# Graph attention on Trainium2: VectorE adds the edge rows to keys and values in one wide instruction, and its four dot products move behind the addition of a finished step's sum

## The chip, the cores and the metric

The kernel runs on one core of one Trainium2 chip. The metric is the device time of one execution in microseconds (us). A core has a matrix engine (TensorE, PE in the rows; its weight loads are PEld), a vector engine (VectorE, DVE), a scalar engine (ScalarE, ACT), GpSimd (POOL), SyncE (SP, used here for DMA issue) and 16 DMA engines. The engines run in order, each on its own queue, and meet through semaphores.

## What is computed

A graph of 6250 nodes and 100000 edges, sorted by destination, passes through one weighted neighbour sum with a residual and a layer norm, and then through two attention convolutions. All of the change lies in the convolutions, which compute, with H = 4 heads of C = 64 channels:

```
q, k, v = x @ Wq + bq, x @ Wk + bk, x @ Wv + bv      # per node
e = edge_attr @ We                                   # per edge
kj = k[src] + e
vj = v[src] + e
logits = einsum('ehc,ehc->eh', q[dst], kj) / sqrt(C)
m = segment_max(logits, dst)
ex = exp(logits - m[dst])
denom = segment_sum(ex, dst)
agg = segment_sum(vj * (ex / denom[dst])[:, :, None], dst)
```

## The kernel before

The program runs five passes one after the other with a barrier between them: the weighted edge pass, a node pass, the attention edge pass of the first convolution (e1), a second node pass, the attention edge pass of the second convolution (e2), and a last node pass. Only `edge_pass_attention` is touched; it is called twice.

An attention pass walks over 832 **steps** of 128 edges each, all edges of a step having their destination in one block of 128 nodes. 26 steps (BATCH) form a **batch** whose softmax is done together, and there are 32 batches. The pass is a software pipeline written out by hand: each engine has its own loop over i, and each step's work is spread over two visits.

In loop round i, the **front** of step i is done:

- GpSimd gathers the 512 numbers of key and value of each edge's source into one of six buffers `kv` (line 1303). It may overwrite a buffer once VectorE's value addition of six steps earlier is done. Every fourth step it also makes the selection matrices `pick` of four steps (line 1294).
- TensorE makes the edge row e (lines 1315 and 1316, in three steps of four; in the fourth it comes ready from memory as `made`) into one of two PSUM banks, and q of the destinations (line 1325) into one of two others.
- VectorE, in `logits(i)`, adds e to the keys (line 1416) and then to the values (line 1420), each 128x256, and makes four dot products of 64 numbers, one for each head (line 1428; each is a product and a short read of the accumulator). The sum of the keys goes to one of two places of `kvj`. The sum of the values goes to one of NV = 44 places, because it is needed much later; so the value addition waits until ScalarE has weighed the step 44 earlier (`weighed`).

The **back** is done LAG = 42 rounds later, when the softmax of the batch is known. In round i ScalarE makes step i-42's mask (lines 1561 and 1567) and weighs its four heads of values (line 1571). TensorE's `sum_up` (line 1366) multiplies the mask by the weighed values of step i-43, into one of two PSUM banks. VectorE's `add_sums` (line 1510) adds the sum of step i-44 to its node block in `acc`. Where that step begins a batch, it first rescales the block (lines 1504 and 1507), and this waits for the same sum. In the text below a step's place is its round modulo 26; since 44 is 18 modulo 26, the rescaling falls on place 18.

Between these, all engines share the batch softmax, by place: a transpose of the logits on TensorE and a scaled copy on ScalarE (place 0, line 1543), two scans on VectorE (place 2, lines 1433 and 1436), further copies and scans (places 6 and 10), the subtraction of the maxima on VectorE (place 12, line 1474), for which ScalarE's exponential waits (place 12, line 1546), and a last transpose and copy (place 14, line 1551). So ScalarE waits for VectorE's `lr` at place 12 of every batch.

VectorE's loop is

```
for i in range(END):
    if i < T:
        logits(i)
    if LATE <= i - LAG < T:
        late_part(i - LAG)
    if 0 <= i - LAG - 2 < T:
        add_sums(i - LAG - 2)
```

followed by the first convolution's skip product (one block of nodes at a time, 49 times in e1), the batch softmax and a small scale update. TensorE's loop runs, in round i: edge row of step i+1, q of step i+1 (which waits for the dots of step i-1), a skip product if due, the softmax transposes, `sum_up(i-43)`.

Of the kernel before, what the change touches and what calls it, by code (L numbers as in the profile page):

```python
# [7 lines left out]
P = 128  # L8
D = 256
H = 4  # L10
C = D // H
# [3 lines left out]
BATCH = 26  # L15
QUAD = 4
# [13 lines left out]
ALU = mybir.AluOpType  # L30
# [1099 lines left out]
def edge_pass_attention(nc, name, k, t, s, w_edge, edge_rows_made, kv_rows, pens, locals16, singles, skip_of):  # L1130
# [10 lines left out]
    T, batches = s.steps, s.batches  # L1141
    LATE = T - LAG
    ident, acc = k["ident"], k["acc"]
    with Phase(nc, name) as ph:
# [17 lines left out]
        if skip_of is not None:  # L1162
# [20 lines left out]
            ph.sems("kv_got", NG), ph.sems("ea_got", NE), ph.sems("runs_got", 2), ph.sems("spots_got", 2))  # L1183
        made_got = ph.sems("made_got", 2)
        w_got, cleared, ones_set = ph.sem("w_got"), ph.sem("cleared"), ph.sem("ones_set")
        e_done, q_done, kj_done, vj_done, dots_done, picked, apart_done = (
            ph.sem(n) for n in ("e_done", "q_done", "kj_done", "vj_done", "dots_done", "picked", "apart_done"))
        flat_done, lr_done, fw_done, mx_inner = (ph.sem(n) for n in ("flat_done", "lr_done", "fw_done", "mx_inner"))
        ends_up, rows_in, outs_done = (ph.sem(n) for n in ("ends_up", "rows_in", "outs_done"))
        across, ends_down, mx_done, less_max = (ph.sem(n) for n in ("across", "ends_down", "mx_done", "less_max"))  # L1190
# [8 lines left out]
        def step_of(a):  # L1199

            return a // (QUAD - 1) * QUAD + a % (QUAD - 1)
# [23 lines left out]
        with nc.Block() as block:  # L1225

            @block.sync
            def _(e):
                tile = Numbers(e, f"{name}_tile", k["tile_row"], s.tiles - 1)

                def load_attrs(a):
                    n = tile.at(step_of(a))
                    if a >= NE:
                        e.wait_ge(e_done, a - NE + 1)
                    e.dma_start(ea[:, a % NE, :], t["attr_tiles"][bass.ds(n, 1), :, :].rearrange("o k c -> (o k) c")
                                ).then_inc(ea_got[a % NE], 16)

                def load_made(c):
                    if c >= 2:
                        e.wait_ge(vj_done, (c - 1) * QUAD)  # L1240
                    e.dma_start(made[:, c % 2, :], edge_rows_made[c * P:(c + 1) * P, :]).then_inc(made_got[c % 2], 16)

                def load_spots(c):
                    if c >= 2:
                        e.wait_ge(picked, c - 1)
                    e.dma_start(spots[:, c % 2, :], locals16[c * QUAD:(c + 1) * QUAD, :].rearrange("s c -> (s c)").unsqueeze(0)
                                .to_broadcast([P, QUAD * P])).then_inc(spots_got[c % 2], 16)

                def load_runs(j):
                    if j == 0:  # L1250
                        e.wait_ge(cleared, 8)
                    if j >= 2:
                        e.wait_ge(mx_done, j - 1)
                    for h in range(H):
                        e.dma_start(pen[ROWS * h + 1:ROWS * h + 1 + BATCH, j % 2, :],
                                    pens[j * BATCH:(j + 1) * BATCH, 0:P + 1]).then_inc(runs_got[j % 2], 16)
                    for way in range(2):
                        e.dma_start(by_head(over[:, j % 2, way, :]),
                                    singles[way:way + 1, j * BATCH:(j + 1) * BATCH].unsqueeze(1)
                                    .to_broadcast([1, H, BATCH])).then_inc(runs_got[j % 2], 16)  # L1260

                e.dma_start(we[:], w_edge).then_inc(w_got, 16)
                load_spots(0)
                for a in range(NE - 1):
                    load_attrs(a)
                load_made(0)
                load_spots(1)
                if skip:
                    skip.load_weights(e)
                for i in range(T):  # L1270
                    c, at = i // QUAD, i % QUAD
                    a = c * (QUAD - 1) + at
                    if at < QUAD - 1 and a + NE - 1 < FRESH:
                        load_attrs(a + NE - 1)
                    if at == QUAD - 1 and c + 1 < s.quads:
                        load_made(c + 1)
                    if i % QUAD == 0 and i // QUAD + 2 < T // QUAD:
                        load_spots(i // QUAD + 2)
                    if i % BATCH == 0:
                        load_runs(i // BATCH)  # L1280
                    if i in due:
                        skip.load(e, due[i] + 1)
                        skip.store(e, due[i])
                if skip:
                    skip.all_stored(e)

            @block.gpsimd
            def _(e):
                def pick_rows(c):

                    e.wait_ge(spots_got[c % 2], 16 * (c // 2 + 1))
                    if c >= 2:
                        e.wait_ge(q_done, (c - 1) * QUAD)
                    e.tensor_scalar(pick[:, c % 2, :], spots[:, c % 2, :], k["own"][:, 0:1], None, ALU.is_equal).then_inc(picked, 1)  # L1294

                e.memset(kvj[:], 1.0).then_inc(ones_set, 1)
                for i in range(T):
                    u = i % NG
                    if i % QUAD == 2:
                        pick_rows(i // QUAD)  # L1300
                    if i >= NG:
                        e.wait_ge(vj_done, i - NG + 1)
                    e.indirect_dma_start(out=kv[:, u, :], out_offset=None,  # L1303
                                         **rows_of(kv_rows, k["src"][:, i:i + 1])).then_inc(kv_got[u], 16)
                e.wait_ge(ones_set, 1)

            @block.tensor
            def _(e):
                chosen = Numbers(e, f"{name}_chosen", k["q_row"], (s.blocks - 1) * D)

                def edge_product(a):
                    e.wait_ge(ea_got[a % NE], 16 * (a // NE + 1))
                    if a >= 2:
                        e.wait_ge(vj_done, step_of(a - 2) + 1)
                    e.matmul(pe_e[a % 2][:, 0:D], ea[:, a % NE, 0:P], we[:, 0, :], start=True, stop=False)  # L1315
                    e.matmul(pe_e[a % 2][:, 0:D], ea[:, a % NE, P:2 * P], we[:, 1, :],  # L1316
                             start=False, stop=True).then_inc(e_done, 1)
# [74 lines left out]
            def _(e):  # L1392
# [7 lines left out]
                if skip:  # L1400
                    skip.make_bias(e)

                def logits(i):
                    j, r = i // BATCH, i % BATCH + 1
                    e.wait_ge(kv_got[i % NG], 16 * (i // NG + 1))
                    c, at = i // QUAD, i % QUAD
                    if at < QUAD - 1:
                        a = c * (QUAD - 1) + at
                        e.wait_ge(e_done, a + 1)
                        edge = pe_e[a % 2][:, 0:D].rearrange("p (h c) -> p h c", h=H)  # L1410
                    else:
                        e.wait_ge(made_got[c % 2], 16 * (c // 2 + 1))
                        edge = made[:, c % 2, :].rearrange("p (h c) -> p h c", h=H)
                    if i >= 2:
                        e.wait_ge(dots_done, i - 1)
                    e.tensor_tensor(kvj[:, i % 2, :, 0:C], kv[:, i % NG, 0:D].rearrange("p (h c) -> p h c", h=H), edge,  # L1416
                                    ALU.add).then_inc(kj_done, 1)
                    if i >= NV:
                        e.wait_ge(weighed, i - NV + 1)
                    e.tensor_tensor(kvj[:, 2 + i % NV, :, 0:C], kv[:, i % NG, D:].rearrange("p (h c) -> p h c", h=H), edge,  # L1420
                                    ALU.add).then_inc(vj_done, 1)
                    e.wait_ge(kj_done, i + 1)
                    e.wait_ge(q_done, i + 1)
                    if j >= 2:
                        e.wait_ge(flat_done, j - 1)
                    for h in range(H):
                        hs = slice(h * C, h * C + C)
                        dot = e.tensor_tensor_reduce(kvj[:, i % 2, h, 0:C], kvj[:, i % 2, h, 0:C], pe_q[i % 2][:, hs], 1.0, 0.0,  # L1428
                                                     ALU.mult, ALU.add, logit[:, j % 2, h, r:r + 1])
                    dot.then_inc(dots_done, 1)  # L1430
# [88 lines left out]

                for i in range(END):  # L1520
                    if i < T:
                        logits(i)
                    if LATE <= i - LAG < T:
                        late_part(i - LAG)
                    if 0 <= i - LAG - 2 < T:
                        add_sums(i - LAG - 2)
                    if i in due:
                        skip.add(e, due[i])
                    j, step = step_at(i)
                    if j is not None:  # L1530
                        softmax(j, step)
                    if 0 <= i - LAG < T:
                        drop_less_one(i - LAG)
# [120 lines left out]
```

## Time and profile before

| | |
|---|---|
| Median of 3 runs | 4820.88 us (4820.83 to 4821.61) |
| The profiled execution's own time | 4832.06 us |
| Its span, first to last instruction | 4830.3 us |
| Busy: TensorE (matmul) | 4189.2 us, 87% |
| Busy: VectorE | 3989.0 us, 83%, 22772 instructions |
| Busy: ScalarE | 2982.2 us, 62% |
| Busy: GpSimd | 3116.4 us, 65% |
| First and last key addition (line 1416) | 1368.7 and 4646.8 us |

The shares are means over six passes. The two attention passes fill most of the span behind 1368.7 us, so the table by stretches of time says more than the totals. The recorded duration of a VectorE instruction is longer than its share of the engine: the next one begins before the last record ends, so the cost of an instruction in a full queue is the distance between two starts.

### The profile page before, as it was taken

Reading aid. Unit: us, or ns where it says so; the run is one execution under the profiler, and the core shown is the slowest. Engines: PE = TensorE matmul, PEld = TensorE weight load, DVE = VectorE, ACT = ScalarE, POOL = GpSimd, SP = SyncE. Lnnn points to the kernel's source line nnn. Section 1 sums busy time; section 2 is a strip of 40 time slices with the busy share of each in tenths; the row PEclk is TensorE's granted clock in tenths of the full one; section 3 lists DMA queues with packets and bytes.
Section 4 is the critical chain, followed back from the end, with each engine's and each line's share of the span. In section 5 each row is a group of like instructions: output and inputs, shape, how many; then the busy total and the mean of one; then the engine's idle time right before and its main releaser. Section 6 shows DMA issues by size and latency. Waiting matters only on the chain. (4 is left out here: it accounts for less than half of the span.)

```text
span 4830.3 us, 107746 instructions
## 1 busy us (share of the span) xinstructions
PE 4189.2 (87%) x17694; PEld 3210.6 (66%) x17694; DVE 3989.0 (83%) x22772; ACT 2982.2 (62%) x10607; POOL 3116.4 (65%) x2996
## 2 busy tenths in 40 slices
PE   2887887888979999999999998889999999999988
PEld 2766666675547777777777774567777777777755
DVE  4655555556869999999999998789999999999986
ACT  1111111112319898989898984149999999989971
POOL 6677777740067777777777771287777777777730
PEclk9999999999999999999999999999999999999989
DMA  4666666654568887878788773587777777777734
GB/s 121 189 192 196 192 193 193 191 167 149 169 212 237 233 236 232 233 229 236 231 234 228 231 230 104 173 247 231 226 230 228 231 228 227 226 228 231 226 114 149
DMA packets 663064, 996.73 MB, mean 206 GB/s; under 512 B 99667, under 2 KB 489690, under 8 KB 662407
## 3 DMA queue, kind: packets, MB, share of 16 engines
q0 software_dynamic: 171408, 540.40, 38.1%
q1 hardware_dynamic: 491000, 449.44, 30.8%
q14 instruction: 471, 3.86, 0.3%
q8 instruction: 185, 3.03, 0.3%
HBM read 870.01 MB, written 119.44 MB: 205 GB/s over the span
## 5 line engine op out<-in xcount | busy, mean ns | idle before, releaser
L1303 POOL DMA_INDIRECT e_kv<-kv,src x1664 | 1635.0, 983 | 748.1 <-DVE e_kvj L1420 449.7
L1571 ACT ACTIVATE e_vals<-e_kvj,e_ex 128x65 f32<-128x65 f32 x6572 | 1725.1, 334 | 5.5 <-PE e_sum L1366 5.1
L1366 PE MATMUL e_sum<-e_vals,e_mask 128*128 128x260 f32 x3328 | 1063.7, 403 | 206.2 <-ACT e_vals L1571 190.0
L1325 PE MATMUL e_q<-q,e_pick 128*128 x3328 | 1017.2, 387 | 95.3 <-DVE e_logit L1428 66.4
L1428 DVE CUSTOM_DVE_ANT_0 e_kvj<-e_kvj,e_q 128x64 f32<-128x64 f32 x6656 | 1060.2, 214 | 3.4 <-PE e_q L1325 2.2
L152 POOL DMA_INDIRECT e_x<-x_rows,e_src x783 | 747.3, 954 | 263.1 <-issue 172.3
L1366 PEld LDWEIGHTS e_sum<-e_vals,e_mask 128*128 128x128 f32 x3328 | 563.0, 190 | 454.4 <-issue 379.7
L1325 PEld LDWEIGHTS e_q<-q,e_pick 128*128 128x128 f32 x3328 | 618.2, 191 | 252.4 <-issue 169.9
L1315 PE MATMUL e_e<-e_we,e_ea 112*128 112x256 f32 x2496 | 752.3, 382 | 17.4 <-DMA e_ea<-attr_tiles 16.2
L1316 PE MATMUL e_e<-e_we,e_ea 112*128 112x256 f32 x2496 | 745.8, 380 | 0.0
L1510 DVE TENSOR_TENSOR acc<-acc,e_sum 128x260 f32 x1664 | 697.3, 419 | 41.4 <-issue 23.6
L530 ACT ACTIVATE q<-e_edges 128x512 f32<-128x512 f32 x208 | 124.2, 597 | 925.5 <-PE e_edges L523 921.7
L1294 POOL TENSOR_SCALAR e_pick<-e_spots,own 128x512 f32<-128x512 bf16 x416 | 660.9, 1589 | 15.4 <-DMA e_spots<-locals 1.1
L1567 ACT ACTIVATE e_mask<-e_apart,one 128x128 f32<-128x128 f32 x1580 | 634.6, 402 | 52.5
L597 PE MATMUL e_sum<-e_x,e_mask 128*128 x1664 | 455.2, 400 | 210.6 <-DVE e_mask L612 114.0
L620 DVE TENSOR_TENSOR acc<-acc,e_sum 128x256 f32 x832 | 349.9, 421 | 332.0 <-PE e_sum L597 308.0
L1561 ACT ACTIVATE e_apart<-iota,local 128x128 f32<-128x128 f32 x1580 | 610.4, 386 | 0.0
L1416 DVE TENSOR_TENSOR e_kvj<-e_kv,e_e 128x256 f32<-128x256 f32 x1248 | 513.4, 411 | 66.2 <-DMA e_kv<-kv,src 40.3
L1315 PEld LDWEIGHTS e_e<-e_we,e_ea 112*128 112x128 f32 x2496 | 477.7, 192 | 96.4 <-issue 20.3
L1420 DVE TENSOR_TENSOR e_kvj<-e_kv,e_e 128x256 f32<-128x256 f32 x1248 | 514.7, 412 | 21.0 <-ACT e_vals L1571 20.6
L1428 DVE DVE_READ_ACCUMULATOR2_ANT e_logit<- 128x1 f32 x6656 | 531.6, 80 | 0.2 <-issue 0.2
L597 PEld LDWEIGHTS e_sum<-e_x,e_mask 128*128 128x128 f32 x1664 | 316.9, 198 | 312.2 <-issue 270.2
(223 smaller groups left out, 4479.1 us busy)
## 6 DMA issues: line engine op xcount, KB each, us to landing
e_ea<-attr_tiles SPq DMA_DIRECT2D x1248, 112.0 KB
edges<-q SPq DMA_DIRECT2D x208, 256.0 KB
e_spots<-locals SPq DMA_DIRECT2D x416, 128.0 KB
e_made<-edges SPq DMA_DIRECT2D x416, 128.0 KB
e_kv<-kv,src POOLq DMA_INDIRECT x1664
kv<-n_proj_rows SPq DMA_DIRECT2D x98, 256.0 KB
q<-attr_tiles SPq DMA_DIRECT2D x208, 112.0 KB
n_x<-x_rows SPq DMA_DIRECT2D x98, 128.0 KB
```

The costliest lines, as they stand in the source:

```text
L152: e.indirect_dma_start(out=self.x[:, at:at + D], out_offset=None, **rows_of(self.t["x_rows"], self.src[:, i:i + 1])).then_inc(self.got[i / ...
L597: e.matmul(sums[i % SUMS][:, 0:D], mask[:, i % R, :], rows, start=True, stop=True).then_inc(summed, 1)
L1294: e.tensor_scalar(pick[:, c % 2, :], spots[:, c % 2, :], k["own"][:, 0:1], None, ALU.is_equal).then_inc(picked, 1)
L1303: e.indirect_dma_start(out=kv[:, u, :], out_offset=None, **rows_of(kv_rows, k["src"][:, i:i + 1])).then_inc(kv_got[u], 16)
L1315: e.matmul(pe_e[a % 2][:, 0:D], ea[:, a % NE, 0:P], we[:, 0, :], start=True, stop=False)
L1316: e.matmul(pe_e[a % 2][:, 0:D], ea[:, a % NE, P:2 * P], we[:, 1, :], start=False, stop=True).then_inc(e_done, 1)
L1325: e.matmul(pe_q[i % 2][:, 0:D], pick[:, c, at:at + P], rows, start=True, stop=True).then_inc(q_done, 1)
L1366: e.matmul(sums[n % 2][:, 0:VALS], mask[:, n % R, :], vals[:, n % R, :], start=True, stop=True).then_inc(summed, 1)
L1428: dot = e.tensor_tensor_reduce(kvj[:, i % 2, h, 0:C], kvj[:, i % 2, h, 0:C], pe_q[i % 2][:, hs], 1.0, 0.0, ALU.mult, ALU.add, logit[:, j % ...
L1510: e.tensor_tensor(rows, rows, sums[n % 2][:, 0:VALS], ALU.add).then_inc(added, 1)
L1567: e.activation(mask[:, n % R, :], apart[:], ACT.Relu, bias=k["one"][:, 0:1], scale=-1.0).then_inc(masked, 1)
L1571: by_weight = e.activation(vals[:, n % R, h * HV:(h + 1) * HV], kvj[:, 2 + n % NV, h, :], ACT.Copy, scale=ex[:, b % 2, h, r:r + 1])
```

## The change

In each step VectorE's two additions of 128x256 become one of 128x512: the gathered row is read as two halves of four heads, the edge row is read twice through a broadcast, and the output goes to the key place and the value place of `kvj`, which one stride joins. The one instruction now waits for what both waited for: the gathered row, the edge row, the dots of two steps earlier, and `weighed`. The semaphores kj_done and vj_done become one, kvj_done, which the gather, the edge product and the loads of `made` now wait for, and the dots as well. `logits` is split in two: `add_edges(i)` stays where it was, and `dots(i)` moves behind `late_part` and `add_sums`, so that a finished step's sum is added between the wide addition and the dots.

```
-                e.tensor_tensor(kvj[:, i % 2, :, 0:C], kv[:, i % NG, 0:D].rearrange("p (h c) -> p h c", h=H), edge,
-                                ALU.add).then_inc(kj_done, 1)
                 if i >= NV:
                     e.wait_ge(weighed, i - NV + 1)
-                e.tensor_tensor(kvj[:, 2 + i % NV, :, 0:C], kv[:, i % NG, D:].rearrange("p (h c) -> p h c", h=H), edge,
-                                ALU.add).then_inc(vj_done, 1)
-                e.wait_ge(kj_done, i + 1)
+                e.tensor_tensor(kvj[:, key_at:value_at + 1:value_at - key_at, :, 0:C],
+                                kv[:, i % NG, :].rearrange("p (a h c) -> p a h c", a=2, h=H),
+                                edge.unsqueeze(1).to_broadcast([P, 2, H, C]), ALU.add).then_inc(kvj_done, 1)
+
+            def dots(i):
+                j, r = i // BATCH, i % BATCH + 1
+                e.wait_ge(kvj_done, i + 1)
                 e.wait_ge(q_done, i + 1)
...
             for i in range(END):
                 if i < T:
-                    logits(i)
+                    add_edges(i)
                 if LATE <= i - LAG < T:
                     late_part(i - LAG)
                 if 0 <= i - LAG - 2 < T:
                     add_sums(i - LAG - 2)
+                if i < T:
+                    dots(i)
```

Here `key_at` is i % 2 and `value_at` is 2 + i % NV. The order of TensorE's instructions, and of the other engines', is the same in both programs; only VectorE's moves. In the rows of order below, L1428 (then L1430) is a head's dot product or its accumulator read, `ISA` without tiles is a register instruction for the block's address, and TENSOR_LOAD reads four steps' addresses from a table.

VectorE, an ordinary step, before:

```order
L1416 TENSOR_TENSOR e_kvj<-e_kv,e_made 128x4x64
L1420 TENSOR_TENSOR e_kvj<-e_kv,e_made 128x4x64
L1428 ISA e_kvj,e_logit<-e_kvj,e_q 128x64
L1428 ISA e_logit 128x1
...
L1510 ISA
L1510 TENSOR_TENSOR acc<-acc,e_sum 128x260
L1416 TENSOR_TENSOR e_kvj<-e_kv,e_e 128x4x64
```

and the same step now:

```order
L1418 TENSOR_TENSOR e_kvj<-e_kv,e_made 128x2x4x64
L1512 ISA
L1512 TENSOR_TENSOR acc<-acc,e_sum 128x260
L1430 ISA e_kvj,e_logit<-e_kvj,e_q 128x64
L1430 ISA e_logit 128x1
...
L1418 TENSOR_TENSOR e_kvj<-e_kv,e_e 128x2x4x64
```

One instruction is gone, and the addition of the sum stands ahead of the eight rows of the dots instead of behind them.

VectorE, the step at place 18, whose block is rescaled first, before:

```order
L1416 TENSOR_TENSOR e_kvj<-e_kv,e_e 128x4x64
L1420 TENSOR_TENSOR e_kvj<-e_kv,e_e 128x4x64
L1428 ISA e_kvj,e_logit<-e_kvj,e_q 128x64
L1428 ISA e_logit 128x1
...
L100 TENSOR_LOAD numbers
L1504 TENSOR_SCALAR e_rescale<-e_sum 128x4
L1507 ISA
L1507 TENSOR_TENSOR acc<-acc,e_rescale 128x260
L1510 TENSOR_TENSOR acc<-acc,e_sum 128x260
```

and now:

```order
L1418 TENSOR_TENSOR e_kvj<-e_kv,e_e 128x2x4x64
L100 TENSOR_LOAD numbers
L1506 TENSOR_SCALAR e_rescale<-e_sum 128x4
L1509 ISA
L1509 TENSOR_TENSOR acc<-acc,e_rescale 128x260
L1512 TENSOR_TENSOR acc<-acc,e_sum 128x260
L1430 ISA e_kvj,e_logit<-e_kvj,e_q 128x64
L1430 ISA e_logit 128x1
```

Here three dependent instructions, the first of which waits for TensorE's sum, now stand ahead of the dots.

## Rows read from the trace of the kernel before

**Rows 1.** Busy time by stretch: start:end, length, PE, PEld, DVE, ACT, POOL, clock, DMA share, GB/s.

```profile
2000.00:2100.00 100.00, 91.35 (x408) 72.75 (x407) 95.30 (x628) 89.10 (x326) 73.53 (x68) 1.00 0.80 234
3500.00:3600.00 100.00, 91.05 (x404) 71.63 (x403) 96.67 (x640) 92.15 (x338) 75.50 (x69) 1.00 0.77 228
```

**Rows 2.** Waits, 3400 to 4600 us: who for whom, us in total, times, longest.

```profile
PE e_sum L1366 <- ACT e_vals L1571: 82.6, 140, 1.7
...
ACT e_lr L1546 <- DVE e_lr L1474: 57.8, 25, 3.3
```

**Rows 3.** Timeline of VectorE, one ordinary step: start us, duration us, instruction [idle before <-releaser].

```profile
3808.01 0.40 DVE L1416 TENSOR_TENSOR e_kvj<-e_kv,e_e 128x256 f32<-128x256 f32 x1
3808.34 0.40 DVE L1420 TENSOR_TENSOR e_kvj<-e_kv,e_e 128x256 f32<-128x256 f32 x1
3808.67 0.20 DVE L1428 CUSTOM_DVE_ANT_0 e_kvj<-e_kvj,e_q 128x64 f32<-128x64 f32 x1
...
3809.23 0.41 DVE L1510 TENSOR_TENSOR acc<-acc,e_sum 128x260 f32 x1
3809.57 0.40 DVE L1416 TENSOR_TENSOR e_kvj<-e_kv,e_e 128x256 f32<-128x256 f32 x1
```

**Rows 4.** Timeline of VectorE in a node pass: an addition of 128x512 from PSUM.

```profile
1257.31 0.67 DVE L744 TENSOR_TENSOR n_proj_rows<-n_proj,n_b_proj 128x512 f32<-128x512 f32 x1
1257.89 0.15 DVE L664 RECIPROCAL n_rs<-n_rs 128x1 f32<-128x1 f32 x1
```

**Rows 5.** Timeline of ScalarE: place 12, one step on, and place 12 again.

```profile
3862.65 0.31 ACT L1546 ACTIVATE e_lr<-e_lr 128x128 f32<-128x128 f32 x1 [2.18 <-DVE e_lr L1474]
3862.86 0.38 ACT L1561 ACTIVATE e_apart<-iota,local 128x128 f32<-128x128 f32 x1
...
3864.55 0.39 ACT L1561 ACTIVATE e_apart<-iota,local 128x128 f32<-128x128 f32 x1
...
3910.71 0.31 ACT L1546 ACTIVATE e_lr<-e_lr 128x128 f32<-128x128 f32 x1 [2.09 <-DVE e_lr L1474]
```

**Rows 6.** Timeline of place 2 in an even batch of e2.

```profile
3890.12 0.42 DVE L1420 TENSOR_TENSOR e_kvj<-e_kv,e_e 128x256 f32<-128x256 f32 x1 [0.21 <-ACT e_vals L1571]
3890.23 0.68 PE L1366 MATMUL e_sum<-e_vals,e_mask 128*128 128x260 f32 x2 [0.40 <-ACT e_vals L1571]
...
3891.11 0.43 DVE L1510 TENSOR_TENSOR acc<-acc,e_sum 128x260 f32 x1
3891.45 0.42 DVE L1433 TENSOR_TENSOR_SCAN e_fw<-e_pen,e_lr 128x128 f32<-128x128 f32 x1
```

**Rows 7.** Timeline of place 2 in an odd batch of e2.

```profile
3841.86 0.42 DVE L1416 TENSOR_TENSOR e_kvj<-e_kv,e_e 128x256 f32<-128x256 f32 x1
3842.07 0.68 PE L1366 MATMUL e_sum<-e_vals,e_mask 128*128 128x260 f32 x2
...
3843.38 0.42 DVE L1510 TENSOR_TENSOR acc<-acc,e_sum 128x260 f32 x1 [0.20 <-issue]
...
3843.72 0.42 DVE L1433 TENSOR_TENSOR_SCAN e_fw<-e_pen,e_lr 128x128 f32<-128x128 f32 x1
```

**Rows 8.** Timeline of place 18 of a batch of e2.

```profile
3920.68 0.71 PE L1366 MATMUL e_sum<-e_vals,e_mask 128*128 128x260 f32 x2
...
3921.49 0.16 DVE L1504 TENSOR_SCALAR e_rescale<-e_sum 128x4 f32<-128x4 f32 x1
...
3922.25 0.42 DVE L1510 TENSOR_TENSOR acc<-acc,e_sum 128x260 f32 x1
...
3922.59 0.44 DVE L1416 TENSOR_TENSOR e_kvj<-e_kv,e_made 128x256 f32<-128x256 f32 x1
```

**Rows 9.** Timeline: TensorE's sum for the step of rows 3, and for a step at place 25.

```profile
3807.47 0.71 PE L1366 MATMUL e_sum<-e_vals,e_mask 128*128 128x260 f32 x2
...
3932.04 0.41 DVE L1416 TENSOR_TENSOR e_kvj<-e_kv,e_e 128x256 f32<-128x256 f32 x1
3932.08 0.60 PE L1366 MATMUL e_sum<-e_vals,e_mask 128*128 128x260 f32 x2
```

More of the change, by code:

```diff
@@ L1185, in edge_pass_attention @@
         w_got, cleared, ones_set = ph.sem("w_got"), ph.sem("cleared"), ph.sem("ones_set")
-        e_done, q_done, kj_done, vj_done, dots_done, picked, apart_done = (
-            ph.sem(n) for n in ("e_done", "q_done", "kj_done", "vj_done", "dots_done", "picked", "apart_done"))
+        e_done, q_done, kvj_done, dots_done, picked, apart_done = (
+            ph.sem(n) for n in ("e_done", "q_done", "kvj_done", "dots_done", "picked", "apart_done"))
         flat_done, lr_done, fw_done, mx_inner = (ph.sem(n) for n in ("flat_done", "lr_done", "fw_done", "mx_inner"))
@@ L1239, in load_made @@
                     if c >= 2:
-                        e.wait_ge(vj_done, (c - 1) * QUAD)
+                        e.wait_ge(kvj_done, (c - 1) * QUAD)
                     e.dma_start(made[:, c % 2, :], edge_rows_made[c * P:(c + 1) * P, :]).then_inc(made_got[c % 2], 16)
@@ L1301, in _ @@
                     if i >= NG:
-                        e.wait_ge(vj_done, i - NG + 1)
+                        e.wait_ge(kvj_done, i - NG + 1)
                     e.indirect_dma_start(out=kv[:, u, :], out_offset=None,
@@ L1313, in edge_product @@
                     if a >= 2:
-                        e.wait_ge(vj_done, step_of(a - 2) + 1)
+                        e.wait_ge(kvj_done, step_of(a - 2) + 1)
                     e.matmul(pe_e[a % 2][:, 0:D], ea[:, a % NE, 0:P], we[:, 0, :], start=True, stop=False)
@@ L1401, in _, with add_edges @@
                     skip.make_bias(e)
-                def logits(i):
-                    j, r = i // BATCH, i % BATCH + 1
+                def add_edges(i):
                     e.wait_ge(kv_got[i % NG], 16 * (i // NG + 1))
+                    key_at, value_at = i % 2, 2 + i % NV
                     c, at = i // QUAD, i % QUAD
```

## Prediction

> **What bounds the kernel now.** I read the table by stretches first, since shares of the whole span mix six passes. In both attention passes VectorE is busy for about 95 to 97 us of 100, TensorE for 91, ScalarE for 89 to 92 [rows 1]. The three are close together, so VectorE leads, but something saved on it can be worth at most what the next engine leaves. GpSimd, at 74 to 76, has room.
>
> The view of waits then says who waits for whom in e2 [rows 2]. ScalarE waits 25 times, once in each batch, for VectorE's subtraction of the maxima, 57.8 us in all, or 2.3 us a batch. TensorE waits 82.6 us for ScalarE's weighed values. So TensorE is no bound by itself.
>
> ScalarE's timeline shows how the two share a batch. Outside the softmax it takes 1.69 us a step with no gap, 3862.86 to 3864.55, and the exponential comes every 48.06 us, each time after a wait of some 2.1 us for VectorE [rows 5]. VectorE takes 1.56 us for an ordinary step [rows 3], less than ScalarE, but has the scans on top. So they take turns. From place 3 to 12 VectorE carries the scans, falls back, and ScalarE waits for it at place 12. Around places 0 to 2 and 14 to 18 VectorE has caught up, and it is held by ScalarE: a value addition sat idle 0.21 us for the weighing 44 steps back [rows 6]. The time of a batch is therefore set by VectorE's path from its last hold at place 2 to the exponential at place 12, and only what is saved between these two comes off the time. What is saved before place 2 ends in the hold.
>
> **The change, part by part.** Against the profiled execution, 4832.1 us, which lies 11.2 us above the median of the runs.
>
> *The wide addition.* Key and value addition now start 0.33 us apart, and the dots 0.33 behind the second: 0.66 us a step [rows 3]. No 128x512 addition from this place is in the trace. The nearest is the node pass's, also with PSUM as an input: the next instruction starts 0.58 us behind it [rows 4]. From its record, 0.67 against 0.40 for 256 columns [rows 3, 4], the distance would be 0.33 + 0.27 = 0.60. I take 0.59, which saves **0.07 us a step**. The bounds are 0.08 and nothing (0.66, if the two halves, the stride and the broadcast cost what the second instruction did). Twice 832 steps at 0.07 would be 116 us if all of it came through.
>
> The Trainium skill (VectorE: DVE Perf Modes, "The DRAIN you can't avoid") says that the next instruction does not start until the pipeline has emptied. By that each addition would cost its whole record. The trace speaks against it here: the value addition starts 0.33 us behind a key addition whose record is 0.40 long [rows 3].
>
> *Waiting for its own result.* The dots now need an addition that has only just been issued, where the key sum had the value addition behind which to finish. The addition of the sum, 0.34 us from start to start [rows 3], lies between, and covers the 0.08 us or so by which a record outlasts its distance. In the first 44 steps of a pass nothing lies between; some 0.1 us a step, but there VectorE has no back work at all and waits for gathers, so I count nothing, and 9 us if that cover is gone.
>
> *The wait for the sum moves ahead of the dots.* This is the part that costs. Before, the sum of step i-44 was needed 1.22 us after the step's start, behind both additions and 0.56 us of dots [rows 3]; now it is needed at 0.59. The dots no longer fill the wait. From the end of TensorE's record to VectorE's start I count 0.20 us (3890.91 to 3891.11) [rows 6].
> - Place 2, even batch. The value addition was held to 3890.12, and the wide one will be held there too. The sum's add can start at 3891.11 as before; but then 0.56 us of dots follow, so the scan at 3891.45 comes **0.56 us late** [rows 6].
> - Place 2, odd batch. The sum's record ends at 3842.75, so its add can start at 3842.95, where before it started at 3843.38, 0.20 of that for issue. With 0.34 and 0.56 the scan comes at 3843.85 against 3843.72: **0.13 late** [rows 7]. The two kinds alternate, mean 0.35.
> - Place 18. Rescaling starts at 3921.49, 0.10 behind the sum's record, and the chain to the next step lasts 1.10 us to 3922.59. The dots, done before it until now, come behind it: **0.56 us late** [rows 8].
> - Places 0, 1 and 14 to 17 are held by ScalarE and TensorE; VectorE's delay there ends in the same holds. Priced at nothing; in the worst case some 0.3 us each.
> - Ordinary steps. In one the sum's record ended 0.17 us after the step's start, so its add is free at 0.37, in time for 0.59; at place 25 it ended 0.64 after, ready at 0.84, and VectorE would wait 0.25 [rows 3, 9]. That one lies just before the hold and is paid by it. From place 3 to 12 VectorE is the later engine, the sums wait for it, and I count nothing.
>
> *The sum.* From place 18 to 2 there are ten steps: 10 x 0.07 = 0.70 saved against 0.56 lost, and the rest ends in the hold at place 2. From place 2 to 12, another ten: 0.70 - 0.35 = **0.35 us a batch**. In e1 the skip product adds to VectorE's work, so that the hold takes less; I put 0.10 more there by choice. Of 32 batches a pass, 30 have both halves of the pipeline: 30 x 0.35 + 30 x 0.45 = 24 us. The waits of the gather, the edge product and `made` for kvj_done fall within 0.1 us of where vj_done was, and GpSimd has room. So 4832.1 becomes 4808, and the median 4820.9 - 24 = **4797 us**.
>
> **The rivals.**
> 1. *The saving comes through.* If the moved waits are absorbed and place 2 is no hard hold, the ceiling is the 116 us of the whole saving, held by ScalarE's 2.3 us a batch of waiting [rows 2], 60 x 2.3 = 138 us. Half of it is likelier than all: about 0.9 us a batch, 4765 us. For it speaks that VectorE is busy most [rows 1]; against it the idle value addition [rows 6]. All of it gives 4705.
> 2. *The dots are missed as cover (slower).* The places are 18 and every plain step up to 12. Per batch 0.56 + 0.35 = 0.91 us is lost and 20 x 0.07 = 1.40 gained. If TensorE's sum comes a mean of (1.40 - 0.91) / 20 = 0.025 us too late for the earlier place in the twenty plain steps, nothing is left; each further 0.025 costs 0.5 us a batch. At 0.05 that is 60 x 0.5 = 30 us, 4851 us. For it: the step at place 25, ready at 0.84 where 0.59 is wanted [rows 9]. Against it: the step of rows 3, ready at 0.37. The same would come of a wide addition at 0.64 instead of 0.59.
> 3. *Nothing measurable.* The hold at place 2 takes more than I count, or the wide addition takes 0.62: 10 x 0.035 - 0.35 = 0. Time 4821 us.
> 4. *Each addition cost its whole record.* As a mechanism of this kernel, two records of 0.40 against one of 0.67 save 0.13 a step [rows 3, 4]: 10 x 0.13 - 0.35 = 0.95 a batch, 57 us, 4764 us. The starts in rows 3 all but exclude it. This is what the rule of the Trainium skill (VectorE: DVE Perf Modes, "The DRAIN you can't avoid") would give; the trace disagrees with it by the 0.33 us named above.
>
> **How the numbers follow.** My forecast, 4780 to 4811, has 0.43; the first rival 0.20 and the fourth 0.03; the second 0.18; the third 0.16. A measurement of this kernel can tell about 0.2%, 10 us, from no change. So faster is 0.43 + 0.20 + 0.03 = 0.66, same 0.16, slower 0.18. The predicted time is the forecast's, 4797 us. The range leaves out the full saving below and the worse half of the second rival above: 4752 to 4836 us.
>
> **What would show it.** The wide addition's next instruction should start 0.58 to 0.60 us behind it. ScalarE's wait at place 12 should fall from 2.3 to about 1.9 us a batch, and the distance of the exponentials by 0.3 to 0.5 us. New idle time should stand ahead of the sum's add and of the rescaling, released by TensorE, at places 2, 14, 16 and 18; and VectorE's busy time should fall by about 1664 x 0.07 = 116 us, whatever becomes of the span. If the waits ahead of the sum's add appear at plain steps from 3 to 12 as well, the second rival is right. If ScalarE's wait at place 12 falls by 1 us or more, the first is. It would be wrong altogether if the wide addition took 0.66 us or more, or if TensorE began to wait for the dots.

## The result, and the profile after

The changed kernel takes 4843.95 us in the median of 5 runs (4841.45 to 4853.52), against 4820.88 us before (4820.75 to 4823.86): a ratio of 1.005, 95% interval 1.0035 to 1.0065. It is **slower by 0.5%**, 23 us, where 24 us less had been forecast, and lies outside the range of 4752 to 4836. The profiled execution took 4843.95 us.

From the page of the changed kernel, the busy times and then VectorE's groups for the wide addition and the sum's add:

```profile
span 4842.2 us, 107658 instructions
...
PE 4192.0 (87%) x17694; PEld 3192.4 (66%) x17694; DVE 3903.1 (81%) x21108; ACT 2985.9 (62%) x10607; POOL 3110.7 (64%) x2996
...
L1418 DVE TENSOR_TENSOR e_kvj<-e_kv,e_e 128x512 f32<-128x512 f32 x1248 | 847.8, 679 | 129.5 <-ACT e_vals L1575 83.9
...
L1512 DVE TENSOR_TENSOR acc<-acc,e_sum 128x260 f32 x1664 | 696.8, 419 | 74.3 <-PE e_sum L1366 51.2
```

VectorE has lost 86 us of busy time (3989.0 to 3903.1; 116 had been forecast) and 1664 instructions, and the program is longer. The work was saved, and idle time has taken more than its place: 129.5 us ahead of the wide addition, most of it for ScalarE, and 74.3 ahead of the sum's add, where TensorE is now named first and before only 41.4 us stood. GpSimd's gathers are not the cause: VectorE waited 46.1 us for them before and 46.4 us now.

The wide addition itself, in a place-10 step of e2 and the one before it:

```profile
3921.41 0.67 DVE L1418 TENSOR_TENSOR e_kvj<-e_kv,e_e 128x512 f32<-128x512 f32 x1
...
3922.01 0.41 DVE L1512 TENSOR_TENSOR acc<-acc,e_sum 128x260 f32 x1
...
3922.89 0.60 PE L1366 MATMUL e_sum<-e_vals,e_mask 128*128 128x260 f32 x2
...
3922.91 0.67 DVE L1418 TENSOR_TENSOR e_kvj<-e_kv,e_e 128x512 f32<-128x512 f32 x1
...
3923.69 0.43 DVE L1512 TENSOR_TENSOR acc<-acc,e_sum 128x260 f32 x1
...
3924.60 0.16 DVE L1467 COPY e_ends<-e_back 128x2 f32<-128x2 f32 x1
```

The first step is as forecast: the sum's add follows 0.60 us behind the wide addition, and the step takes 1.50 us where it took 1.56 [rows 3]. In the second, TensorE's sum ends at 3923.49, VectorE is free at 3923.50, and its add starts only at 3923.69, 0.20 us behind the sum's end and 0.78 behind the wide addition. From the wide addition to the copy of the ends the step needs 1.69 us. The next two fences are the kernel before at the same place and the changed kernel's waits.

```profile
3904.35 0.60 PE L1366 MATMUL e_sum<-e_vals,e_mask 128*128 128x260 f32 x2
...
3904.61 0.40 DVE L1416 TENSOR_TENSOR e_kvj<-e_kv,e_e 128x256 f32<-128x256 f32 x1
...
3905.84 0.41 DVE L1510 TENSOR_TENSOR acc<-acc,e_sum 128x260 f32 x1
...
3906.18 0.14 DVE L1465 COPY e_ends<-e_back 128x2 f32<-128x2 f32 x1
```

Before, the same stretch took 1.57 us. TensorE's sum ended at 3904.95, 0.34 behind the step's start, and was not needed until 1.23. Now it ends 0.58 behind the start, so that its add can begin at 0.78, and it is needed at 0.59. So this step, between place 2 and 12, lost 0.12 us where I had counted a gain of 0.07. It is no exception: over the batches of e2 the round at place 10, its scans included, grew from 2.67 to 2.78 us in the mean, while those at places 7 and 8 fell by 0.07 and 0.06.

Waits of the changed kernel, 3400 to 4600 us (who for whom, us in total, times, longest):

```profile
PE e_sum L1366 <- ACT e_vals L1575: 68.6, 111, 1.4
ACT e_lr L1550 <- DVE e_lr L1476: 58.0, 25, 2.9
DVE e_kvj L1418 <- ACT e_vals L1575: 36.8, 63, 1.0
PE e_q L1325 <- DVE e_logit L1430: 29.5, 52, 1.1
DVE acc L1512 <- PE e_sum L1366: 17.7, 78, 0.6
DVE e_rescale L1506 <- PE e_sum L1366: 13.4, 25, 0.6
```

ScalarE's wait for the maxima is 58.0 us, as good as the 57.8 before [rows 2]: nothing of the saving reached place 12. TensorE's wait for the dots, 29.5 us now, was 16.9 us in the same stretch before:

```profile
PE e_q L1325 <- DVE e_logit L1428: 16.9, 30, 0.9
```

And one wait stands in the changed trace that no part of the forecast had named, ScalarE's for the small scale update at place 14. The line's own view, first before, then after:

```profile
L1554 ACT ACTIVATE e_scale<-e_scale x64: 188/204/206, 1441.9 to 4668.0; 1x4 f32<-1x4 f32 x64
...
  DVE e_scale L1485: 3.3, 7
```

```profile
L1558 ACT ACTIVATE e_scale<-e_scale x64: 187/204/206, 1439.6 to 4689.2; 1x4 f32<-1x4 f32 x64
...
  DVE e_scale L1487: 17.8, 33
```

It grew by 14.5 us over the whole span. One such place 14 of e2:

```profile
3930.92 0.39 ACT L1565 ACTIVATE e_apart<-iota,local 128x128 f32<-128x128 f32 x1
...
3931.14 0.69 DVE L1418 TENSOR_TENSOR e_kvj<-e_kv,e_e 128x512 f32<-128x512 f32 x1 [0.67 <-ACT e_vals L1575]
3931.16 0.68 PE L1366 MATMUL e_sum<-e_vals,e_mask 128*128 128x260 f32 x2 [0.99 <-ACT e_vals L1575]
...
3932.04 0.43 DVE L1512 TENSOR_TENSOR acc<-acc,e_sum 128x260 f32 x1 [0.20 <-PE e_sum L1366]
...
3932.38 0.21 DVE L1430 CUSTOM_DVE_ANT_0 e_kvj<-e_kvj,e_q 128x64 f32<-128x64 f32 x1
...
3933.12 0.22 DVE L1487 TENSOR_SCALAR e_scale<-e_scale,goes_on 1x4 f32<-1x4 f32 x1
...
3933.37 0.21 ACT L1558 ACTIVATE e_scale<-e_scale 1x4 f32<-1x4 f32 x1 [0.51 <-DVE e_scale L1487]
```

The wide addition waits for ScalarE, the sum's add waits for TensorE, the four dots come behind both, then the scale update, and ScalarE, which is the engine that VectorE was waiting for, now stands still 0.51 us for it.

To see where the time is, I take the exponentials of e2 from the third batch to the last. Before:

```profile
3290.51 0.31 ACT L1546 ACTIVATE e_lr<-e_lr 128x128 f32<-128x128 f32 x1 [2.55 <-DVE e_lr L1474]
...
4664.57 0.31 ACT L1546 ACTIVATE e_lr<-e_lr 128x128 f32<-128x128 f32 x1 [3.17 <-DVE e_lr L1474]
```

and after:

```profile
3304.80 0.31 ACT L1550 ACTIVATE e_lr<-e_lr 128x128 f32<-128x128 f32 x1 [2.29 <-DVE e_lr L1476]
...
4686.14 0.31 ACT L1550 ACTIVATE e_lr<-e_lr 128x128 f32<-128x128 f32 x1 [3.17 <-DVE e_lr L1476]
```

1374.06 us have become 1381.34, +7.3 us over 29 batches; the same view of e1 gives +11.7. The spans differ by 11.9 us only, less than the medians, since the profiled execution of before had been 11 us above its median; from its last exponential to its end it took 165.7 us against 156.1, at a mean granted clock of 0.88 against 0.92.

A batch can be cut in two at the end of ScalarE's weighing that releases VectorE at place 2. These are the means of 28 batches of each convolution, from the starts and ends in the two traces, with the standard error of the difference:

| Stretch | e1 before, after | e2 before, after | forecast |
|---|---|---|---|
| From that weighing to the next exponential (places 2 to 12) | 21.47, 21.45 us: -0.02 ± 0.08 | 20.88, 20.85 us: -0.02 ± 0.04 | -0.45 and -0.35 |
| From the exponential to that weighing (places 12 to 2) | 27.20, 27.67 us: +0.48 ± 0.06 | 26.86, 27.15 us: +0.29 ± 0.05 | nothing |

The stretch from which all of the gain was to come is as long as before. What has grown is the other one, and in it ScalarE's idle time ahead of the scale update alone grew by 0.27 and 0.26 us a batch.

### The profile page after: what moved, and what is told of

Its sections match the earlier page's. It is cut to its first block and busy times, and to the rows that moved or that the text cites. A ratio compares the mean times of both kernels' runs of the same rounds, so it can differ in the third digit from the quotient of the medians.

```text
span 4842.2 us, 107658 instructions
## 1 busy us (share of the span) xinstructions
PE 4192.0 (87%) x17694; PEld 3192.4 (66%) x17694; DVE 3903.1 (81%) x21108; ACT 2985.9 (62%) x10607; POOL 3110.7 (64%) x2996
## 5 line engine op out<-in xcount | busy, mean ns | idle before, releaser
L1430 DVE CUSTOM_DVE_ANT_0 e_kvj<-e_kvj,e_q 128x64 f32<-128x64 f32 x6656 | 1064.6, 215 | 7.8 <-PE e_q L1325 2.8
L1418 DVE TENSOR_TENSOR e_kvj<-e_kv,e_e 128x512 f32<-128x512 f32 x1248 | 847.8, 679 | 129.5 <-ACT e_vals L1575 83.9
L1325 PEld LDWEIGHTS e_q<-q,e_pick 128*128 128x128 f32 x3328 | 602.1, 190 | 332.5 <-issue 252.2
L1512 DVE TENSOR_TENSOR acc<-acc,e_sum 128x260 f32 x1664 | 696.8, 419 | 74.3 <-PE e_sum L1366 51.2
L1315 PEld LDWEIGHTS e_e<-e_we,e_ea 112*128 112x128 f32 x2496 | 476.4, 192 | 93.3 <-issue 18.7
L1430 DVE DVE_READ_ACCUMULATOR2_ANT e_logit<- 128x1 f32 x6656 | 537.4, 81 | 0.2
L1316 PEld LDWEIGHTS e_e<-e_we,e_ea 112*128 112x128 f32 x2496 | 471.3, 189 | 69.7
```

What stands on the lines that cost most here:

```text
L1325: e.matmul(pe_q[i % 2][:, 0:D], pick[:, c, at:at + P], rows, start=True, stop=True).then_inc(q_done, 1)
L1418: e.tensor_tensor(kvj[:, key_at:value_at + 1:value_at - key_at, :, 0:C], kv[:, i % NG, :].rearrange("p (a h c) -> p a h c", a=2, h=H), edg ...
L1512: e.tensor_tensor(rows, rows, sums[n % 2][:, 0:VALS], ALU.add).then_inc(added, 1)
```

## The experiments

The standing theory, A: the waits for TensorE's sum, which now stand ahead of the dots, cost more than the wide addition saves. A1 puts the cost at place 14 (and 2), A2 at the plain places through TensorE. The rivals: B, the wide addition's own start is held by `weighed`; C, the keys suffer because they now wait for `weighed` with the values. In the three sets of runs below the kernel before took 4825.6, 4826.8 and 4824.0 us, 3 to 6 us more than in the first; each ratio is against the set's own runs, and differences of a few us between sets say nothing. The change itself was run in the first set only, so each difference from it below, taken between medians, is uncertain by those 3 to 6 us.

**One part alone.** `wide_only` keeps the wide addition, with the dots directly behind it and the sum's add last:

```
                     if i < T:
                         add_edges(i)
+                        dots(i)
...
                         add_sums(i - LAG - 2)
-                    if i < T:
-                        dots(i)
```

> The wide addition alone; the dots follow it directly and the sum's add comes last, as before the change. Theory A (the moved dots are what costs): the wide addition saves about 0.08 us a step and the bare wait for its own result gives about that back (a record of 0.68 us against a distance of 0.58), so 4815 to 4835 us, with no new idle time ahead of the sum's add. Theory B (the wide addition's later start, held by weighed, is what costs): at least as slow as the change, 4840 us or more.

4892.59 us, ratio 1.0133 (1.0116 to 1.0151): slower than the change by 49 us, in B's range of 4840 or more and far from A's. A was wrong on the size: I had counted the bare wait as giving back the saving and no more. Its timeline:

```profile
3804.70 0.68 DVE L1418 TENSOR_TENSOR e_kvj<-e_kv,e_e 128x512 f32<-128x512 f32 x1
3805.41 0.22 DVE L1430 CUSTOM_DVE_ANT_0 e_kvj<-e_kvj,e_q 128x64 f32<-128x64 f32 x1
...
3805.99 0.42 DVE L1512 TENSOR_TENSOR acc<-acc,e_sum 128x260 f32 x1
```

The dots start 0.71 behind the wide addition, 0.03 behind its record's end, and not 0.66 as they did behind the key addition [rows 3]. The four dots then take 0.58, so that the sum's add comes at 1.29 where it came at 1.22. So the wide addition without something between it and the dots is a loss by itself; the second half of the change is what makes the first usable. The traces bear this out: from the weighing to the next exponential a batch takes 0.92 us more than before in both convolutions, about 0.09 a step. Since this wait for its own result is absent from the change, where the sum's add stands between, the run speaks neither for A nor for B as the cause there, although its number is one that B had asked for.

**The other part alone.** `order_only` has the two additions of before, and the sum's add between them and the dots:

```
-                def logits(i):
-                    j, r = i // BATCH, i % BATCH + 1
+                def add_edges(i):
...
+
+                def dots(i):
+                    j, r = i // BATCH, i % BATCH + 1
                     e.wait_ge(kj_done, i + 1)
...
-                        logits(i)
+                        add_edges(i)
...
                         add_sums(i - LAG - 2)
+                    if i < T:
+                        dots(i)
```

> The two additions of before, with the sum's add between them and the dots. Theory A: all of the change's losses and none of its saving of 0.08 us a step; ten to twenty steps a batch count, 60 batches, so 48 to 95 us above the change, 4890 to 4940 us. Theory B: near 4821 us, since the key addition isn't held.

4866.8 us, ratio 1.0078 (1.0058 to 1.0098). B is out as the whole cause: nothing of this version's keys is held, and it is 41 us slower than the kernel before. But A had asked for 48 to 95 us above the change, and it is 23. So **the move of the dots costs about 41 us, and the wide addition, once it stands in the new order, is worth 23**, not the 116 us of 0.07 in every step and not the 48 of ten steps a batch. In the traces it is a gain of 0.2 us a batch between the weighing and the exponential, which just makes good what the moved dots lose there, and of 0.07 in the other stretch. The waits of `order_only` in the same 1200 us:

```profile
DVE acc L1512 <- PE e_sum L1366: 39.3, 75, 0.9
...
DVE e_rescale L1506 <- PE e_sum L1366: 11.9, 25, 0.9
```

**Where the dots' place matters.** `first14` puts the dots ahead of the sum's add at place 14 only, `firstheld` at places 2, 14, 16 and 18:

```
+                    dots_first = i % BATCH in (2, 14, 16, 18)
                     if i < T:
                         add_edges(i)
+                        if dots_first:
+                            dots(i)
...
-                    if i < T:
+                    if i < T and not dots_first:
                         dots(i)
```

> The change, but at place 14 of each batch the dots come ahead of the sum's add, where ScalarE's second exponential (of scale) waits for VectorE. Theory A1 (that wait, new in the trace, 0.25 us a batch, is the added time): 15 to 19 us off the change, 4825 to 4829 us, and ScalarE's wait for scale falls from 6.3 us to under 1 us in 1200 us. Theory A2 (the loss lies between places 3 and 12, where TensorE's q and sum come late behind the later dots): within 5 us of the change, 4839 to 4849 us.

> The change, but at places 2, 14, 16 and 18, where the sum is late, the dots come ahead of the sum's add. Theory A1: place 2 brings back 0.35 us a batch on top of place 14's 0.3, so 35 to 40 us off the change, 4804 to 4809 us. Theory A2: half of that at most, 4825 us or more, since the later dots at the plain places still delay TensorE.

4833.91 us for `first14`, ratio 1.0018 (1.0008 to 1.0028), and 4825.69 for `firstheld`, 0.9996 (0.9987 to 1.0006). Place 14 gives 10 us back (15 if each is taken against its own set's kernel before), where A1 asked 15 to 19 and A2 allowed 5; the four places together 18 us (23), half of A1's 35 to 40 and just at A2's bound. In the traces nearly all of it lies between the exponential and the weighing: that stretch falls by 0.14 and 0.17 us a batch (e1, e2) in `first14` and by 0.31 and 0.19 in `firstheld`. Neither account had all of it: ScalarE still waits 12.1 us for the scale in `first14`, against 17.8 and 3.3:

```profile
  DVE e_scale L1487: 12.1, 33
```

since the wide addition still starts late there (0.66 us of idle time for ScalarE at place 14, as in the change) and the dots still wait for its result. What is shown is that the order at four of 26 places decides the sign: with it turned back there, the change is the time of the kernel before.

**The keys' hold.** `room` has 45 value places instead of 44, paid for with one buffer of attributes; `room_before` is its control, and `firstheld_room` joins it with the dots first:

```
-    NV, NG, NE, R = LAG + 2, 6, 5, 4
+    NV, NG, NE, R = LAG + 3, 6, 4, 4
```

> The change with 45 value places instead of 44 (four buffers of attributes instead of five make the space), so that weighed, one step earlier, no longer holds the wide addition. Theory A (the sum's wait ahead of the dots is the cost): the sum is as late as before, so within 5 us of the change, 4839 to 4849 us, with the idle time only moved from the wide addition to the sum's add. Theory C (the keys, now tied to the values' wait for weighed, are the cost): 0.3 us at place 2 and at place 14, some 25 us off, near 4819 us.

> The kernel before with the same 45 value places and four buffers of attributes: the control. Both theories: 0 to 8 us below the kernel before, 4813 to 4821 us, since its value addition is held 0.1 to 0.25 us at places 2, 14 and 16; over 4826 us would say that the fourth buffer of attributes was needed.

> The dots first at places 2, 14, 16 and 18, and 45 value places. There the wide addition's start decides, no longer the sum. Theory A with C: 0.2 us at place 2 and 0.25 at place 14 off the version with 44 places (4825.7), 15 to 27 us, so 4799 to 4811 us, below the kernel before. If the hold by weighed costs nothing here either: 4826 us.

4853.08 us (ratio 1.0051, 1.0034 to 1.0068), 4832.41 (1.0014, 1.0003 to 1.0024) and 4831.38 (1.0009, 0.9999 to 1.002). The control is over its 4826 us, so the fifth buffer of attributes is worth some 6 us or more and blurs all three. With 6 us taken off, `room` stands in A's range and far from C's 4819, and `firstheld_room` at the 4826 us that it was given for a hold that costs nothing; its other forecast, 4799 to 4811, was missed by 20 us or more. To leave the buffers alone, `room_lag` gets the extra place from LAG = 41 with the buffers as they were:

```
-    LAG = BATCH + 8 * PACE
-    NV, NG, NE, R = LAG + 2, 6, 5, 4
+    LAG = BATCH + 8 * PACE - 1
+    NV, NG, NE, R = LAG + 3, 6, 5, 4
```

> The change with LAG of 41: the hold by weighed gone without a buffer less, which blurred the run named room. Theory A (the sum's wait dominates): within 5 us of the change, 4839 to 4849 us. Theory C (the keys tied to weighed are the cost): near 4820 us.

4835.97 us, ratio 1.0027 (1.0015 to 1.0038): 8 us below the change, 3 below A's range and far from C's 4820. Its waits show why:

```profile
ACT e_lr L1550 <- DVE e_lr L1476: 56.2, 25, 2.9
DVE acc L1512 <- PE e_sum L1366: 54.2, 81, 1.3
```

The 36.8 us of waits for `weighed` are gone, and the sum's wait went from 17.7 to 54.2 us. Who takes one hold away finds the other: most of the idle time has only moved. C is a part at most, 8 us of the 23 (11 against its own set); how much of that comes of the shorter LAG by itself is open, since the kernel before was not run with LAG = 41.

**The sum a step older.** `late_sums` is the change with each round adding the sum of step i-45:

```
-                    if 0 <= i - LAG - 2 < T:
-                        add_sums(i - LAG - 2)
+                    if 0 <= i - LAG - 3 < T:
+                        add_sums(i - LAG - 3)
```

with END one round later.

> The change, but each round adds the sum of step i-45 instead of i-44, which TensorE has had a step longer. Theory A: the waits ahead of the sum's add and the rescaling go (17.7 and 13.4 us in 1200 us), place 2 gives 0.4 us and place 14 0.3 us a batch back: 4795 to 4810 us. Rival: with two PSUM banks TensorE's next sum now waits for the later release, its queue with it, and the time stays at 4840 us or rises.

**4810.75 us, ratio 0.9966 (0.9952 to 0.998)**: 33 us below the change and 0.3% faster than the kernel before. The waits of the same 1200 us:

```profile
DVE e_kvj L1418 <- ACT e_vals L1575: 46.4, 76, 0.9
ACT e_lr L1550 <- DVE e_lr L1476: 45.5, 25, 2.4
...
DVE acc L1512 <- PE e_sum L1366: 0.6, 2, 0.3
```

The wait ahead of the sum's add has fallen from 17.7 us to 0.6, the one ahead of the rescaling no longer shows, and ScalarE's wait at place 12 fell from 58.0 to 45.5 us. From the weighing at place 2 to the next exponential a batch is now 0.26 us (e1) and 0.54 us (e2) shorter than in the kernel before: here is the gain that the forecast had looked for. The other stretch is still 0.38 us longer than before in e1, and 0.05 in e2. The dots stand where they stand in the change, and yet TensorE's wait for them, 29.5 us there, no longer shows either; so it was not the later dots as such that cost. This is the wait of theory A taken away by one edit, and it is worth more than the whole loss.

Its two controls: `late_before` does the same to the kernel before, `late_order` to `order_only`.

> The kernel before, with each round adding the sum of step i-45: the control for late_sums. Theory A (the wait for the sum costs only where the dots no longer cover it): here the dots cover it already but for the rescaling at one place a batch, so 4810 to 4822 us against 4822 to 4827 of the kernel before. Rival (a later sum is worth as much in any order, and says nothing on the change): 30 us or more below the kernel before, 4795 us.

> Two additions, the dots behind the sum's add, the sum a step older: late_sums (4810.8 us) without the wide addition. Theory A: what is left between the two is the 0.07 to 0.08 us a step of the wide addition over the ten steps from place 2 to 12 of 60 batches, 42 to 48 us, so 4850 to 4860 us. If the hold at ScalarE takes most of it: 4820 to 4835 us.

`late_before` took **4986.94 us, ratio 1.0338 (1.0316 to 1.0361)**, 163 us more. Both expectations were wrong, and in the direction that neither had. Its timeline:

```profile
3803.14 0.42 DVE L1510 TENSOR_TENSOR acc<-acc,e_sum 128x260 f32 x1
3803.49 0.41 DVE L1416 TENSOR_TENSOR e_kvj<-e_kv,e_e 128x256 f32<-128x256 f32 x1
...
3803.67 0.68 PE L1366 MATMUL e_sum<-e_vals,e_mask 128*128 128x260 f32 x2 [0.64 <-issue]
...
3804.71 0.42 DVE L1510 TENSOR_TENSOR acc<-acc,e_sum 128x260 f32 x1
...
3805.23 0.68 PE L1366 MATMUL e_sum<-e_vals,e_mask 128*128 128x260 f32 x2 [0.46 <-issue]
```

TensorE's sum of round i needs the bank that the add of step i-45 frees, and that add now comes last in VectorE's round, behind the dots. Each sum on TensorE starts 0.1 us behind the end of such an add (3803.56 to 3803.67, 3805.13 to 3805.23), after 0.46 to 0.64 us of idle time, and the next edge row stands behind it. In `late_sums` the add comes 0.6 us into the round, early enough. So the sum's place and its age belong together: last in the round with step i-44, or early in the round with step i-45. The change had moved the one and not the other. The view gives only "issue" for this idle time, so that it is this bank's is read from the starts. They agree over the whole trace: of 688 sums that TensorE starts after standing idle, 493 start 0.08 to 0.13 us behind the end of such an add, with 252 of 357 us of idle time; in `late_sums` it is 89 of 404, with 43 of 198 us.

`late_order` took 4833.61 us, ratio 1.0018 (1.0008 to 1.0028), in the case that the hold at ScalarE takes most. Against `late_sums` the wide addition is worth 23 us, the same as between `order_only` and the change, and the older sum is worth 33 us with either addition. Two pairs with one answer: of the 0.07 to 0.08 us a step, 116 to 133 us in 1664 steps, a fifth to a sixth comes through.

**The best version.** `late_lag` joins `late_sums` and LAG = 41.

> late_sums with LAG of 41 instead of 42, so that the 44 value places are one step more than is needed and weighed no longer holds the wide addition (46.4 us of waits in 1200 us of late_sums). If that hold lies on the path: 15 to 25 us below late_sums, 4786 to 4796 us. If ScalarE's own pace is what it stands for: within 5 us of late_sums, 4806 to 4816 us.

**4801.93 us, ratio 0.9951 (0.9933 to 0.9969)**: 0.5% faster than the kernel before and the fastest here. It lies 9 us below `late_sums`, between the two expectations. The hold by `weighed` is gone from its waits, but 49.0 us of idle time stand ahead of the wide addition all the same, now spread over more places and with no releaser named:

```profile
DVE e_kvj L1418 <- issue: 49.0, 129, 1.0
ACT e_lr L1550 <- DVE e_lr L1476: 46.9, 25, 2.4
```

So 46.4 us of waits were worth 9. What the new idle time waits for was not found.

## Why the prediction was wrong

Two terms of the sum failed. From place 2 to 12 it had a gain of 0.35 us a batch (0.45 in e1), and 0.02 came, since TensorE's sum, which VectorE now needs ahead of the dots, was late at plain steps that had been priced at nothing; from place 12 to 2 it had nothing, and 0.29 us (0.48 in e1) were lost, most of it in ScalarE's wait for the scale update at place 14. By term:

- *The wide addition.* Right: where nothing is awaited, the next instruction starts 0.58 to 0.60 us behind it, and steps of 1.50 us stand where 1.56 stood. Rival 4 is out. The section of the Trainium skill behind that rival (VectorE: DVE Perf Modes, "The DRAIN you can't avoid") goes on to say that a next instruction which nothing holds starts earlier; the 0.33 us of rows 3 fit that, so the trace does not disagree with the section as a whole, as the prediction has it. The busy time fell by 86 us and not by the 116 of the forecast; why was not worked out.
- *Waiting for its own result.* Right for the change, where the sum's add covers it. I had put a price of 9 us on the first 44 steps of a pass without it; `wide_only` shows what it is worth over all steps: with the cover gone the kernel is 49 us above the change and 67 above the kernel before.
- *Place 2.* The loss was forecast at 0.35 us a batch. An even batch of e2 in the changed kernel is shown below this list: the wide addition is held to 3908.40 and the scan starts at 3910.20, 1.80 behind it, where before it started 1.33 behind the held value addition [rows 6]. The expected 0.56 is 0.47 there. Right in kind and near in size.
- *Ordinary steps from place 3 to 12: the step that failed first.* I wrote that VectorE is the later engine there, that the sums wait for it, and counted nothing. The ten steps were to give 0.70 us. The sum's add waited at plain steps too: at place 10 the sum ended as late as it was needed and 0.12 us was lost instead. The ten rounds gave 0.45 us in e2 and 0.25 in e1, and ScalarE's wait at place 12 stayed at 58.0 us, so the whole stretch only paid for place 2. I had taken one step, with its sum ready at 0.37, for all ten; in the trace of before the sum at place 10 of e2 ended 0.32 us behind the step's start in the mean, ready at 0.52, a margin of 0.07 us. `late_sums`, without the wait, has the gain.
- *Places 14 to 17: the step that failed second, and where the kernel got slower.* "VectorE's delay there ends in the same holds. Priced at nothing; in the worst case some 0.3 us each." At place 14 ScalarE itself waits for VectorE's scale update, behind the dots: 3.3 us before, 17.8 after, 0.26 us a batch more, and `first14` gave 10 us back. This is a wait that I had not looked for, since before it was nearly empty.
- *Place 18 and the steps behind it.* Not tested apart. The rescaling waits 13.4 us in 25 batches, 0.54 each, for TensorE's sum, which is the 0.56 us of the dots that had filled it. The rounds at places 19 to 25 and 0 gave 0.3 us where eight times 0.07 would be 0.56.
- *The rivals.* The second had the sign, half of the mechanism and 4851 us, against 4844; it had 0.18. Its test, idle time ahead of the sum's add at plain steps from 3 to 12, was met in small: 0.10 us at place 10 and 0.05 at place 6 of e2 in the mean. But its 4851 us were reckoned with 0.05 us of waiting at each plain step, and the traces have some 0.03 lost at each, which by its own sum gives some 5 to 10 us and not 30. Most of the rest is place 14, which it lacked; that its number lies so near is in part luck. The first, with 0.20, was nowhere near.
- *The signs.* Idle time ahead of the sum's add at places 2, 14 and 16, and ahead of the rescaling, released by TensorE, came as said, though part of it is old: at places 2, 14 and 16 of e2 it is 0.16 to 0.21 us a batch, where 0.12 to 0.14 stood before. The last sign, that TensorE begins to wait for the dots, was ill chosen: it did so before the change too, 16.9 us, and does so more now, 29.5.
- *The range* ended at 4836 because I left out the worse half of the second rival, and the result fell there.

Place 2 of an even batch of e2, changed kernel:

```profile
3908.40 0.69 DVE L1418 TENSOR_TENSOR e_kvj<-e_kv,e_e 128x512 f32<-128x512 f32 x1 [0.49 <-ACT e_vals L1575]
3908.41 0.68 PE L1366 MATMUL e_sum<-e_vals,e_mask 128*128 128x260 f32 x2 [0.40 <-ACT e_vals L1575]
...
3909.29 0.43 DVE L1512 TENSOR_TENSOR acc<-acc,e_sum 128x260 f32 x1 [0.21 <-PE e_sum L1366]
...
3910.20 0.42 DVE L1435 TENSOR_TENSOR_SCAN e_fw<-e_pen,e_lr 128x128 f32<-128x128 f32 x1
```

The sum's add starts 0.20 us behind the end of TensorE's record, as in rows 6, and all four dots stand behind it.

## What to carry to other kernels

When a wait is moved ahead of work that used to cover it, give what it waits for one stage more, and check that the resource freed by it is still freed early enough for the producer: here the same delay of one step made one order 33 us faster and the other 163 us slower. An engine that is 95% busy with two neighbours at 90% [rows 1] gave back only a small part of what was saved on it (23 us of 116 to 133 here). Before a delay is priced at nothing because "it is held anyway", list who waits for that engine in just that stretch, even where the wait is still empty. And before one step is taken for ten, see how late the awaited result comes in each of them.

## What was not expected of the hardware

In `wide_only` the first dot, which waits for the wide addition just ahead, starts 0.03 us behind the end of its record (0.71 against 0.68 for 512 columns), in nearly every step of the trace; in the change the sum's add, which does not, starts 0.07 us ahead of that end (0.60 against 0.67). So the wait for the neighbour's result cost 0.11 us, more than the 0.07 that the saved instruction gave.
